# Gated attention block: whole weight loads, small loads as rows, and sums of layer two's weights moved between engines

## The reference

```python
def _L0_xattn_ref(query, key, value, Wq, Wk, Wv, Wo, bq, bk, bv, bo):
    Q = split_heads(query @ Wq + bq)
    K = split_heads(key @ Wk + bk)
    V = split_heads(value @ Wv + bv)
    scores = jnp.einsum('bhqd,bhkd->bhqk', Q, K) * scale
    attn = jax.nn.softmax(scores, axis=-1)
    ctx = jnp.einsum('bhqk,bhkd->bhqd', attn, V)
    ...
    return ctx @ Wo + bo
def _L0_ffn_ref(x, k0, k1, k2, s0, s1, s2):
    h = jnp.concatenate([x, -x], axis=-1)
    h = s0 * _conn_dense(k0, h)        # 1024 -> 2048
    h = jax.nn.relu(h) * 2
    h = s1 * _conn_dense(k1, h)        # 2048 -> 2048
    h = jax.nn.relu(h) * 2
    h = s2 * _conn_dense(k2, h)        # 2048 -> 512
    return h
x = x + jnp.tanh(g_xattn[0]) * _L0_xattn_ref(_layernorm(x), ctx, ctx, Wq, Wk, Wv, Wo, bq, bk, bv, bo)
x = x + jnp.tanh(g_ffn[0]) * _L0_ffn_ref(_layernorm(x), k0, k1, k2, s0, s1, s2)
```

## Time and profile before

| | us |
|---|---|
| three runs: lowest, median, highest | 1517.25, 1518.82, 1519.34 |
| the profiled execution | 1519.47 |
| its span, first to last instruction | 1517.7 |
| PE busy in the span | 1492.7 (98%) |
| PEld, DVE, ACT, POOL busy | 1367.3 (90%), 1148.0 (76%), 780.4 (51%), 170.3 (11%) |

### The profile page before, as it was taken

One profiled execution on the slowest core, in us unless ns is written; L12 is line 12 of the kernel. 1 busy time (PEld: TensorE's weight loads), 2 busy tenths in 40 slices (PEclk: granted clock), 3 DMA queues, 4 the chain that ended last, 5 costly groups with the idle time before them and its releaser, 6 DMA issues.

```text
span 1517.7 us, 48349 instructions
## 1 busy us (share of the span) xinstructions
PE 1492.7 (98%) x20600; PEld 1367.3 (90%) x20600; DVE 1148.0 (76%) x2270; ACT 780.4 (51%) x1696; POOL 170.3 (11%) x281
## 2 busy tenths in 40 slices
PE   7899999999999999999999999999999999999999
PEld 5597898999999898998999999898999989999897
DVE  5888699777787777777778786777768777787653
ACT  4552554636456464654646466464654636465431
POOL 3202011020100102010020101102010010201000
PEclk9999999999999999999999999999999999999999
DMA  9652242432425243254443424244252533424200
GB/s 263 125 105 58 46 106 58 109 68 70 89 53 104 57 99 68 52 107 73 98 71 78 79 54 103 57 103 67 56 114 50 99 65 78 78 54 103 30 30 16
DMA packets 284118, 121.09 MB, mean 80 GB/s; under 512 B 249728, under 2 KB 267136, under 8 KB 283904
## 3 DMA queue, kind: packets, MB, share of 16 engines
q1 hardware_dynamic: 282128, 118.01, 36.8%
q10 hardware_dynamic: 1776, 0.01, 0.1%
HBM read 37.76 MB, written 16.78 MB: 36 GB/s over the span
## 4 chain that ended last, share of the span: by engine, by line
PE 91%; DVE 5%; DMA 2%; issue 1%; ACT 1%; SPq 0%; POOL 0%; DVEq 0%; ACTq 0%
PE bank L1608 23%; PE bank L1609 23%; PE bank L1634 11%; PE bank L1554 7%; PE bank L1555 7%; PE bank L1486 2%; PE bank L1541 2%; PE bank L1487 2%; PE bank L1543 2%; PE bank L1488 2%; PE bank L1469 2%; PE bank L1470 2%; PE bank L1471 2%; PE bank L1515 2%; PE bank L1479 1%
## 5 line engine op out<-in xcount | busy, mean ns | idle before, releaser
L1608 PE MATMUL bank<-H,W 128*128 128x128 f16 x6720 | 777.4, 219 | 1.6 <-DVE H L1136 1.2
L1609 PE MATMUL bank<-H,W 128*128 128x128 f16 x6720 | 777.4, 219 | 0.0
L1608 PEld LDWEIGHTS bank<-H,W 128*128 128x128 fp8e5 x6720 | 656.6, 98 | 5.3 <-DVE H L1136 1.5
L1609 PEld LDWEIGHTS bank<-H,W 128*128 128x128 fp8e5 x6720 | 657.4, 98 | 2.9
L1554 PE MATMUL bank<-hT,W 128*128 128x256 f16 (+1 forms) x1040 | 228.7, 271 | 1.6 <-issue 1.1
L1555 PE MATMUL bank<-hT,W 128*128 128x256 f16 (+1 forms) x1040 | 228.7, 271 | 0.0
L1634 PE MATMUL bank<-W,h 128*128 128x256 fp8e5 x1624 | 208.0, 273 | 1.1 <-DVE R L1186 0.5
L1141 DVE TENSOR_TENSOR C<-bank,C 128x256 f32<-128x256 f32 x240 | 101.1, 422 | 141.6 <-PE bank L1609 118.9
L735 POOL TENSOR_TENSOR xn<-pvs 128x128 f32<-128x128 f32 x120 | 59.7, 497 | 1045.0 <-DVE pvs L1108 1045.0
L1634 PEld LDWEIGHTS bank<-W,h 128*128 128x128 f16 x1624 | 154.5, 98 | 21.1 <-DVE R L1186 1.2
L803 ACT ACTIVATE Pf<-bank,nmax 128x128 f32<-128x128 f32 x496 | 141.2, 370 | 36.2 <-DVE nmax L1095 23.0
(11 more groups left out here) (151 smaller groups left out, 2047.2 us busy)
## 6 DMA issues: line engine op xcount, KB each, us to landing
Qst<-q_bounce SPq DMA_DIRECT2D x120, 128.0 KB, 2.8
Y<-in_x_dram SPq DMA_DIRECT2D x16, 512.0 KB, 3.6
R<-X SPq DMA_DIRECT2D x16, 512.0 KB, 3.3
q_bounce<-Qhl SPq DMA_DIRECT2D x120, 64.0 KB
out_dram<-R SPq DMA_DIRECT2D x15, 512.0 KB, 4.2
W<-in_L_ffn_k_dram SPq DMA_DIRECT2D x10, 512.0 KB, 7.2
W<-in_L_ffn_k_dram SPq DMA_DIRECT2D x2, 1024.0 KB, 13.7
PT<-Phl SPq DMA_TRANSPOSE x120, 3.1
```

Of the source, the lines that this page charges most:

```text
L1608: mm(o, w, H0[:, 0, i, b_of, :], start=first, stop=False, skip_group_check=True)
L1609: last = mm(o, w, H0[:, 1, i, b_of, :], start=False, stop=i == PAIRS - 1, skip_group_check=True)
```

## The change

1. **Whole loads.** SP's order becomes: tokens, all of Wq, context, all of Wk, then as before. `load_half`, `key_tile`, `key_place` and `query_weights` go; the key tiles come in plain order; the low part of Wq is made for 512 columns at once, and the first query matmul waits for all four pieces.
2. **Small loads as rows.** ACT's seven loads become five scalars of one element each, into one row, and two biases as four rows of 512 bytes. A new item SMALL on PE transposes the eight bias rows and spreads the scalar row by a matmul with a row of ones; ACT copies `bk_c`, `bq_c` and `scal` out of that bank.
3. **A new `FIRST`.** Layer norm, Wq and the queries come first, keys 0 and 1 right behind them; keys 2 to 7 move in between the units of the attention. SCALARS comes ahead of KM 1. CT 0 comes ahead of the last PV.
4. **S3 on GpSimd.** In chunk one S3 of each group of `W1` is made by POOL (`weight_difference`), as one instruction over 2048 elements; DVE's S2 waits for it through `w1_s3`. `W2`'s S3 stays on DVE.
5. **Two quartered sums whole.** S1 and S2 of group 3, made in chunk two in four quarters each, are made whole in slots 48 and 49 of chunk one.
6. A few items in `WEAVE_0` and `WEAVE_1` move by a slot or within one.

```diff
@@ SP's loads
-            load(ctx_f, ctx.rearrange("(b p) d -> p b d", p=P), ctx_in)
-            load_half(Wk_f, Wk, 0, wk_in)
-            load(Y_flat, x_v[0], x_loaded)
-            load_half(Wq_f, Wq, 0, wq_in)
-            load_half(Wk_f, Wk, 1, wk_in)
-            load_half(Wq_f, Wq, 1, wq_in)
+            load(Y_flat, x_v[0], x_loaded)
+            load(Wq_f, by_rows(Wq), wq_in)
+            load(ctx_f, ctx.rearrange("(b p) d -> p b d", p=P), ctx_in)
+            load(Wk_f, by_rows(Wk), wk_in)
@@ ACT's loads
-                load(bk_c[:, :], bk.rearrange("(k p) -> p k", p=P), bk_in)
-                load(bq_c[:, :], bq.rearrange("(k p) -> p k", p=P), bq_in)
             for n, s in enumerate((g_xattn, g_ffn, s0, s1, s2)):
-                load(scal[:, n:n + 1], to_all(s, 1), scalars_in)
+                load(scal_row[:, n:n + 1], s.rearrange("(a n) -> a n", a=1), scalars_in)
+            load(bias_rows[0:KT, :], bk.rearrange("(k p) -> k p", p=P), bias_in)
+            load(bias_rows[KT:2 * KT, :], bq.rearrange("(k p) -> k p", p=P), bias_in)
@@ ACT and PE, new item
+                if kind == "SMALL":
+                    act.wait_ge(small_turned, 1)
+                    bank = banks[FIRST_BANK[item]]
+                    nc.scalar.activation(bk_c[:, :], bank[:, 0:KT], ACT.Copy, scale=SCALE)
+                    nc.scalar.activation(bq_c[:, :], bank[:, KT:2 * KT], ACT.Copy)
+                    nc.scalar.activation(scal[:, :], bank[:, 2 * KT:2 * KT + 5], ACT.Copy).then_inc(small_made, 1)
...
+                if kind == "SMALL":
+                    pe.wait_ge(ident_made, 1)
+                    pe.wait_ge(bias_in, 32)
+                    turn(bank[:, 0:2 * KT], bias_rows, ident[0:2 * KT, 0:2 * KT])
+                    pe.wait_ge(ones_made, 1)
+                    pe.wait_ge(scalars_in, 5 * 16)
+                    mm(bank[:, 2 * KT:2 * KT + 5], ones_row, scal_row, start=True, stop=True).then_inc(small_turned, 1)
@@ POOL, new
+            def weight_difference(q, step):
+                if q < GROUPS and step == 1:
+                    pool.wait_ge(w1_signs, q + 1)
+                    pool.tensor_tensor(W1[:, q, A_S3], W1[:, q, 0], W1[:, q, 2], ALU.subtract,
+                                       saturate=False).then_inc(w1_s3, 1)
@@ weight_step
-                if step == 1:
-                    if third:
-                        dve.wait_ge(w2_made, 1)
-                    else:
-                        dve.wait_ge(w1_signs, q + 1)
+                if step == 1 and third:
+                    dve.wait_ge(w2_made, 1)
                     V_.tensor_tensor(S3, L11, L21, ALU.subtract, saturate=False).then_inc(made, through)
@@ LATE_WEIGHTS
         9: [(0, 0)],
+        11: [(0, 1)],
         17: [(1, 0)],
-        18: [(0, 1)],
+        18: [(1, 1)],
...
-        24: [(0, 3)],
-        25: [(1, 1)],
+        24: [(2, 1), (0, 3)],
...
+        42: [(3, 1)],
+        48: [(3, 2)],
+        49: [(3, 3)],
@@ PARTS: (3, 2, *) and (3, 3, *) in slots 25 to 32 go; (4, 3, *) and (4, 4, *) move back by three and one
```

More of the change, by code:

```diff
@@ L345, in gated_block_kernel @@
     FIRST_BANK.update((item, 6 + n % 2)
-                      for n, item in enumerate(i for i in FIRST_ITEMS if i[0] in ("CX", "Q", "K", "T2")))
+                      for n, item in enumerate(i for i in FIRST_ITEMS if i[0] in ("SMALL", "CX", "Q", "K", "T2")))
     def user_before(items, bank, item):
@@ L453, in gated_block_kernel @@
             sem(n) for n in ("w0_step", "w0_made", "w2_made", "w2_sums", "w2_back"))
-        w1_signs, w1_made = sem("w1_signs"), [sem(f"w1_made{q}") for q in range(GROUPS)]
+        w1_signs, w1_s3, w1_made = sem("w1_signs"), sem("w1_s3"), [sem(f"w1_made{q}") for q in range(GROUPS)]
         x_loaded, r_copied, out_stored = sem("x_loaded"), sem("r_copied"), sem("out_stored")
@@ L743, in _ @@
                 for s in range(len(SLOTS)):
+                    for part in LATE_WEIGHTS.get(s, []) if f == 0 else []:
+                        weight_difference(*part)
                     for ahead, item in woven(s, f):
@@ L750, in load @@
                 act.dma_start(to, source).then_inc(semaphore, 16)
-            with nc.allow_non_contiguous_dma(reason="two biases of 2 KiB, one feature per row"):
-                load(bk_c[:, :], bk.rearrange("(k p) -> p k", p=P), bk_in)
-                load(bq_c[:, :], bq.rearrange("(k p) -> p k", p=P), bq_in)
             for n, s in enumerate((g_xattn, g_ffn, s0, s1, s2)):
-                load(scal[:, n:n + 1], to_all(s, 1), scalars_in)
+                load(scal_row[:, n:n + 1], s.rearrange("(a n) -> a n", a=1), scalars_in)
+            load(bias_rows[0:KT, :], bk.rearrange("(k p) -> k p", p=P), bias_in)
+            load(bias_rows[KT:2 * KT, :], bq.rearrange("(k p) -> k p", p=P), bias_in)
             def prepare(item):
                 kind, n = item
+                if kind == "SMALL":
[4 more added lines that the diff above has]
+                    nc.scalar.activation(scal[:, :], bank[:, 2 * KT:2 * KT + 5], ACT.Copy).then_inc(small_made, 1)
                 if kind == "CX":
@@ L765, in prepare @@
                 if kind == "KP":
-                    b, m = key_tile(n)
+                    b, m = divmod(n, KT)
                     if n == 0:
-                        act.wait_ge(bk_in, 16)
-                        nc.scalar.activation(bk_c[:, :], bk_c[:, :], ACT.Copy, scale=SCALE).then_inc(bk_scaled, 1)
-                        act.wait_ge(bk_scaled, 1)
+                        act.wait_ge(small_made, 1)
                     act.wait_ge(k_done, n + 1)
@@ L781, in prepare @@
                 if kind == "CQ":
-                    act.wait_ge(wq_in[n // 2], 16)
-                    hi, _, source = query_weights(n)
-                    nc.scalar.activation(hi, source, ACT.Copy, scale=WS).then_inc(wq_hi, 1)
+                    act.wait_ge(wq_in, 16)
+                    nc.scalar.activation(Wq_hi[:, n, :], Wq_f[:, n, :], ACT.Copy, scale=WS).then_inc(wq_hi, 1)
                 if kind == "CO":
@@ L1279, in prepare @@
                     dve.wait_ge(wq_hi, n + 1)
-                    hi, lo, source = query_weights(n)
-                    V_.scalar_tensor_tensor(out=lo, in0=source, scalar=WS, in1=hi, op0=ALU.mult, op1=ALU.subtract)\
+                    V_.scalar_tensor_tensor(out=Wq_lo[:, n, :], in0=Wq_f[:, n, :], scalar=WS,
+                                            in1=Wq_hi[:, n, :], op0=ALU.mult, op1=ALU.subtract)\
                         .then_inc(wq_lo, 1)
@@ L1316, in weight_step @@
                 S1, S2, S3, S4 = (Wg[:, b, pairs] for b in (A_S1, A_S2, A_S3, A_S4))
-                ahead = (step - 1) * 4 if not third else 8 * (parts[0] // 2) + 2 * (step - 1)
+                ahead = (step - 2) * 4 if not third else 8 * (parts[0] // 2) + 2 * (step - 1)
                 if third and step == 0:
@@ L1339, in weight_step @@
                 if step == 3:
-                    dve.wait_ge(made, ahead - (2 if third else 4))
+                    if third:
+                        dve.wait_ge(made, ahead - 2)
+                    else:
+                        dve.wait_ge(w1_s3, q + 1)
                     V_.tensor_tensor(S2, L22, S3, ALU.subtract, saturate=False).then_inc(made, through)
@@ L1583, in feed @@
                     if f == 1 and s == P1:
[L1584 removed]
+                        pe.wait_ge(w1_made[n], 12)
+                        pe.wait_ge(w1_s3, n + 1)
                     if s == P1 and n == 0:
```

77 lines of the change are left out of this document (30 added, 47 removed), and 68 rows, old and new, of tables (FIRST, WEAVE_0, WEAVE_1).

## The result

The changed kernel takes 1521.60 us in the median of 20 runs (1519.28 to 1524.94); the kernel before takes 1518.64 in 20 runs beside it (1517.17 to 1519.76). The ratio of the means is 1.0021, with a 95% interval of 1.0015 to 1.0027: 3.0 us slower, where 1.0 us faster was predicted, and clear of no difference. Its runs also lie twice as far apart. The profiled execution of after is one of the quicker half, 1521.01 (span 1518.9), against 1519.47 (span 1517.7) of before.

A forecast was written before the change was run, and what follows sets the result against it. PE was taken to bound nearly everything behind 65 us, leaving gains only at the start and the DVE-bound piece around 200 to 220. Terms -2.1 + 1.6 - 0.5 = -1.0 us gave 1517.8 us, likeliest range 1514.3 to 1521.5.

The forecast's parts named there:

- Loads, first queries, tiny instructions: Start: first query matmul 4 us earlier, SCALARS up to 2 more; 3.3 us counted at SP's load of tokens.
- the small rows: Start: 13 packets issued by about 4.5 us, needed by 8; no loss taken; late-landing rival 1519.9, chance 0.14.
- The clock at the start: Start: a low PE clock would take 2.4 to 3 of 3.3 us; middle taken, 2.1 us earlier, ends 0 and 4.5.
- SP's queue: End of the start: 20 us of DMAs stand behind SP's load of tokens, and the first layer's ReLU waits for them.
- S3 on POOL: Chunk one: POOL's S3 shuts out DVE, PE idles near 97 for 0.9 to 2.3 us; 1.6 us loss taken.
- two whole sums at nothing: Chunk one: 4.4 us of sums ahead of chunk two's first layer-one pairs cost 0, or 1 us without cover.
- S3 of the fourth group: About 142 to 146.5: holds the second layer norm, but PE has work until 157, so no loss.
- Quarters out of 200 to 220: DVE between 207 and 226: eight quarters of about 0.6 us leave; 0.5 us won, between 0 and 1.
- The sum: Whole kernel: -2.1 + 1.6 - 0.5 = -1.0 us, giving 1517.8 against the median 1518.82.
- The rival on the slower side: Chunk one: POOL's sums hold PE at several PVs, low clock at the start; +4.5 - 0.9 gives 1522.4, chance 0.14.

The follow-up runs named there:

- loads_only: After with the weave tables, LATE_WEIGHTS, PARTS and weight_step of before and no S3 on POOL; loads, small rows and FIRST stay changed: 1518.64 us, ratio 1.0000.
- before_whole: The kernel before with only the two sums made whole, in slot 49 of chunk one: 1517.28 us, ratio 0.9990.
- quarters_back: The kernel after with S1 and S2 of the fourth group in quarters in chunk two again, S3 still on POOL: 1523.7 us, ratio 1.0035.
- the two halves: New loads, small rows and FIRST alone: ratio 1.0000; before with S3 on POOL, whole sums and new weave tables alone: ratio 1.0012.

## Why the prediction was wrong, step by step

- **Loads, first queries, tiny instructions: the mechanism held.** Tokens 4.2 (predicted 5.3), N1 8.0 (9.2), first query 13.60 (13.4), the tiny instructions at 0.14 to 0.41 us, exponents at 23.08 (21.1). That 13.4 was hit so closely is in part luck. The tokens and N1 were 1.1 to 1.2 us ahead of the prediction and Wq had landed at 7.4 instead of 8.3, but the small rows landed at 8.2 only. PE's transposes, whose tokens were ready at 8.0, started behind SMALL at 8.80, and ACT's first piece of Wq at 9.08. By an estimate from these rows, some 1 us of the first query's time is the small rows'; the prediction took no loss for them, and no run tests it.
- **The clock at the start: the term that was mis-sized.** The prediction took the middle between a low and a high clock, 2.1 us. The first matmul on `W0` did come 2.63 earlier in after's profile (62.57), but by the mean of the eleven traces against that of the four it is 0.46, and the median of loads_only says 0 within 1.2 us. Of the 4.0 us between forecast and result this term is the largest part, 1.6 to 2.1. Where the clock stayed high, the working was right: in loads_only's trace SP's load of tokens went out at 44.42 (predicted 44.1). Three things were missed. The rows were read from a profile of before that ended its start at 65.20, the latest of the four, with low stretches at 28 to 31 and at 52 to 55. The new start has low stretches too, in eight of eleven traces, at the first of two places or at both, and both together cost 4.2 to 4.4 us (66.75 against 62.57, 64.84 against 60.46). And SP's queue takes its share: the load of tokens went out at 46.53 instead of 47.37, and what stands behind it took 19.7 us to the first layer's ReLU at 66.22, as the prediction said; 2.63 us at 62 were 1.26 at 74, the rest went into the two waits that grew.
- **S3 on POOL: right in kind, short in size.** The lock is there, with 3.46, 3.78 and 5.48 us on DVE beside POOL. The sum takes 3.83 us, inside the bounds of 3.4 and 4.5. PE lost 2.05 where 1.6 stood. It did not lose it at the PV: the row maximum and the exponents behind the locked low part hold a bank, and PE's next scores come before its next PV. With one chance in three of the clock's 1.65, an estimate from two traces of six, the term is 2.6.
- By the Trainium skill, "GPSIMD Engine Reference", section "Elementwise — side-by-side cycle accounting", a two-input float32 instruction over 2048 elements takes 4.5 us; no run here has that form, and the float8 one took 3.83. The lock that the Trainium skill has in "SBUF — State Buffer", section "SBUF: two separate sides", agrees with the three DVE rows beside POOL's sums: they end 0.3, 0.5 and 2.1 us behind POOL, and alone they take 0.42, 0.69 and 2.28.
- **The step that failed: two whole sums at nothing.** The prediction let 4.4 us of DVE run ahead of "chunk two's first layer-one pairs" and looked for its reader there. The sum in slot 48 stands ahead of something nearer: the low part of layer two's last half in chunk one, for which the second pair on `W0` of chunk two waits. It cost 1.64 to 1.69 us in the four traces with POOL's fourth S3, 0.67 in the two without it, and nothing in slot 49. DVE's idle time in that stretch was real (1.61 us just ahead of this low part in before_whole), but the sum in slot 48 was not behind the waiting instruction; it was ahead of it. S3 of the fourth group was also put at nothing ("PE has work until 157"); it is 1.0 of the 1.64.
- **Quarters out of 200 to 220: right in kind, the size open.** From SP's second copy of the residual to its third took 90.1 us in the mean of eleven traces with whole sums (89.1 to 90.5) and 91.3 in that of seven with quarters (90.55 to 92.4, before's own the shortest): 1.2 us where 0.5 stood. The two groups differ in the weave tables and the start too. Kernels that differ in these sums and their slots alone give 0.85 (before, 90.55, and before_whole, 89.70) and 0.1 to 0.5 (quarters_back, 90.6, and the two traces of after, 90.5 and 90.1).
- **The sum** with the sizes from the traces: -0.4 (the start) + 2.6 + 1.6 - 1.2 + 0.3 (outside the span) = +2.9 us, against 3.0 (2.3 to 4.1) measured. With 0.5 for the quarters it is 3.6. That it comes out so close proves little, as the medians of the two halves give 1.5. The rival on the slower side named 1522.4 and POOL's sums at several PVs; the time was near, the mechanism wasn't: one place, at the scores, and the other stall from a sum on DVE itself.

## What to carry to other kernels

An instruction put into an in-order engine's idle time is free only if it stands behind the next instruction that somebody waits for: look for the first reader behind its slot, not for the next one of its own kind. A start that is freed on one engine hands its gain to the queue that ends last; read that queue from the freed point to the first consumer before counting the gain. The price of an idle stretch of PE is not its length alone. And a single profile of the kernel before is one draw: read a start from several before taking a gain from it.
